# A constant of the cross-attention output added by VectorE, and one softmax pass over 16 heads

## The reference

```python
x = x + _L0_attn_ref(_layernorm(x), w_qkva, gamma)            # gated linear scan over the 1024 tokens
x = x + _L0_xattn_ref(_layernorm(x), ctx, Wq, Wkv, null_kv, Wout, ln_scale, ln_bias)
x = x + _L0_ffn_ref(_layernorm(x), w_gate, w_up, w_down)      # silu(gate) * up, both quantised, then down
```

```python
k = concatenate((nk, k)); v = concatenate((nv, v))            # 65 keys and values for each head
attn = softmax(q @ k.T)                                       # max over 65 scores, exp, sum, divide
out = (attn @ v) reshaped to (tokens, 16 * 64) @ Wout         # 256 channels
out = (out - mean) * rsqrt(var + 1e-6) * ln_scale + ln_bias
```

## Time and profile before

| what | value |
|---|---|
| median of 3 runs | 495.2 us |
| the profiled execution's own time | 493.31 us |
| its span | 491.5 us |
| between span and time | 1.8 us |
| PE busy | 461.3 us |
| DVE busy | 402.8 us |
| ACT busy | 329.0 us |
| POOL busy | 308.8 us |
| granted clock, mean share of full speed | 0.994 |

### The profile page before, as it was taken

How to read it: one execution, slowest core, us unless ns; L and a number is a source line. 1 busy time by engine, 2 the same in 40 slices (tenths; PEclk the granted TensorE clock), 3 DMA queues, 4 the chain that set the end, 5 groups by cost and what they waited for, 6 DMA issues and landing times.

```text
span 491.5 us, 7915 instructions
## 1 busy us (share of the span) xinstructions
PE 461.3 (94%) x2504; PEld 361.7 (74%) x2532; DVE 402.8 (82%) x882; ACT 329.0 (67%) x429; POOL 308.8 (63%) x465
## 2 busy tenths in 40 slices
PE   1999999999999999999999999999999999999673
PEld 0777888787677788777778777878878777786432
DVE  4689988974555688998989989899898998997785
ACT  4556644144544344898888888889788888887551
POOL 2234555741011478897788787787877878888860
PEclk9999999999999999999999999999999999999989
DMA  8997000240000000012131121212222121222243
GB/s 261 325 373 280 3 0 1 43 87 1 1 1 1 1 0 7 12 27 59 39 54 40 39 59 39 55 39 44 54 44 49 40 58 40 44 49 60 48 107 98
DMA packets 67129, 31.72 MB, mean 65 GB/s; under 512 B 49680, under 2 KB 65296, under 8 KB 67088
## 3 DMA queue, kind: packets, MB, share of 16 engines
q1 hardware_dynamic: 67088, 31.21, 25.2%
HBM read 15.21 MB, written 4.19 MB: 39 GB/s over the span
## 4 chain that ended last, share of the span: by engine, by line
PE 83%; DVE 6%; POOL 5%; issue 2%; DMA 2%; ACT 2%; SPq 0%; POOLq 0%; DVEq 0%; ACTq 0%
PE psum L1285 37%; PE psum L1301 12%; PE psum L1564 10%; PE psum L1559 10%; PE psum L1536 3%; PE psum L1544 2%; PE psum L1389 2%; PE psum L1425 2%; PE psum L1406 2%; PE psum L1320 2%; PE psum L1336 1%; DMA gcol<-in_L_attn_gamma_dram 1%; DVE region_a L1008 1%; DVE region_c L1111 1%; PE psum L1556 1%
## 5 line engine op out<-in xcount | busy, mean ns | idle before, releaser
L577 POOL TENSOR_TENSOR region_d<-region_d,rden 128x1024 f32<-128x1024 f32 x30 | 57.1, 1904 | 13.4 <-DVE rden L1087 13.1
L1559 PE MATMUL psum<-VW,region_d 128*128 128x256 f32 x256 | 60.6, 380 | 0.2
L1564 PE MATMUL psum<-VW,region_d 128*128 128x256 f32 x256 | 60.5, 379 | 0.0
L1071 DVE TENSOR_REDUCE mx<-psum 128x8 f32<-128x512 f32 x64 | 44.0, 687 | 14.3 <-PE psum L1285 13.2
L1285 PE MATMUL psum<-Mhi,xT2hi 128*128 128x512 f32 x128 | 53.8, 420 | 0.7 <-DVE xT2lo L1053 0.6
L1564 PEld LDWEIGHTS psum<-VW,region_d 128*128 128x128 f32 x256 | 48.6, 190 | 6.6
L1111 DVE SCALAR_TENSOR_TENSOR region_c<-psum,hzw,region_c 128x1024 f32<-128x1024 f32 x32 | 41.1, 1283 | 12.9 <-ACT region_c L791 12.7
L1559 PEld LDWEIGHTS psum<-VW,region_d 128*128 128x128 f32 x256 | 46.3, 190 | 6.5 <-ACT region_d L862 0.6
L1285 PE MATMUL psum<-Mhi,xT2lo 128*128 128x512 f32 x128 | 50.3, 393 | 0.0
L1285 PE MATMUL psum<-Mlo,xT2hi 128*128 128x512 f32 x128 | 50.0, 390 | 0.0
L1076 DVE SCALAR_TENSOR_TENSOR region_d<-mx,psum 128x512 f32<-128x512 f32 x60 | 40.9, 681 | 1.0
(11 more groups left out here) (160 smaller groups left out, 1164.3 us busy)
## 6 DMA issues: line engine op xcount, KB each, us to landing
out_dram<-xs SPq DMA_DIRECT2D x32, 128.0 KB, 1.9
xs<-in_x_dram SPq DMA_DIRECT2D x1, 2560.0 KB, 13.2
VW<-in_L_xattn_Wkv_dram SPq DMA_DIRECT2D x1, 2048.0 KB, 12.9
region_b<-in_L_xattn_Wkv_dram SPq DMA_DIRECT2D x1, 2048.0 KB, 16.8
xs<-in_x_dram SPq DMA_DIRECT2D x3, 512.0 KB, 6.7
region_w<-in_L_ffn_w_gate_dram SPq DMA_DIRECT2D x2, 512.0 KB, 9.6
region_w<-in_L_ffn_w_up_dram SPq DMA_DIRECT2D x2, 512.0 KB, 7.8
region_w<-in_L_ffn_w_down_dram SPq DMA_DIRECT2D x8, 128.0 KB, 5.7
```

Source lines behind the costliest of these rows:

```text
L577: pool.tensor_tensor(p_of(t).rearrange("p (h j) -> p h j", j=MK), e[:, :, 0:MK], rden[:, v, :].unsqueeze(2).broadcast_to([P, H, MK]), ALU. ...
L1071: dve.tensor_reduce(mx[:, hh, :], scores, AX.X, ALU.max).then_inc(max_done, 1)
L1559: pe.matmul(bank(7, D), pT[:, pair, :], VW[:, batch(n), pair, :], start=False, stop=False)
L1564: mm = pe.matmul(bank(7, D), pT[:, pair, :], VW[:, batch(n), pair, :], start=False, stop=pair == HC - 1)
```

## The change

The product of `ones_r` and `vnull` on PE goes. `vnull` becomes a plain float32 tile with the whole constant in all 128 rows (`nvsel` gets the null value in all its columns, and the subtraction L1102, the constant `ones_r` and a zeroing go). DVE adds `vnull` to bank 7 on the way to `y2` and takes the statistics from `y2`; ACT's `norm_out` works in place in `y2`. PE waits for DVE's addition of the tile before (`out_whole`) and no longer for ACT's normalisation (`y2_ready`). The wait on `x2_done` moves from ACT to DVE. In steps 5 to 29 (tiles 7 to 31) one `softmax_whole` stands for two `softmax_half`: one maximum over two banks, one null column, one subtraction, after both halves of the scores.

```diff
--- before.py
+++ after.py
@@ -77,8 +77,7 @@
 
 
         NR = P
-        vnull = sbuf("vnull", [NR, D], F32R)
-        ones_r = sbuf("ones_r", [NR, P], F32R)
+        vnull = sbuf("vnull", [NR, D])
         wgT = sbuf("wgT", [P, KD, FI], BF16)
         wuT = sbuf("wuT", [P, KD, FI], BF16)
         wdT = sbuf("wdT", [P, FC, D], BF16)
@@ -259,7 +258,6 @@
         wqT0_ready = sem("wqT0_ready")
         wqT1_ready = sem("wqT1_ready")
         nulls_negated = sem("nulls_negated")
-        nvsel_zero = sem("nvsel_zero")
         wout_summed = sem("wout_summed")
         fT_psum = sem("fT_psum")
         kvT_ready = sem("kvT_ready")
@@ -271,8 +269,8 @@
         xT2_lo_ready = sem("xT2_lo_ready")
         nv_set = sem("nv_set")
         vnull_psum = sem("vnull_psum")
-        vnull_hi = sem("vnull_hi")
         vnull_ready = sem("vnull_ready")
+        out_whole = sem("out_whole")
         absum_done = sem("absum_done")
         tot_psum = sem("tot_psum")
         wscale_done = sem("wscale_done")
@@ -510,8 +508,6 @@
                 pool.affine_select(out=t[:, :], in_=t[:, :], compare_op=ALU.not_equal, fill=1.0, base=0,
                                    pattern=[[-1, P]], channel_multiplier=1).then_inc(ident_set, 1)
             pool.memset(ones[:, :], 1.0).then_inc(consts_set, 1)
-            pool.memset(ones_r[:, :].bitcast(F32), 1.0).then_inc(consts_set, 1)
-            pool.memset(nvsel[:, :], 0.0).then_inc(nvsel_zero, 1)
             pool.wait_ge(consts_set, 2)
 
             def rounded(i):
@@ -546,9 +542,7 @@
                     rounded(2)
 
             groups(stage1)
-            pool.wait_ge(nvsel_zero, 1)
-            for row in (0, DH // 2):
-                pool.tensor_copy(nvsel[:, row:row + 1], nulls[:, 1:2]).then_inc(nv_set, 1)
+            pool.tensor_copy(nvsel[:, :], nulls[:, 1:2].broadcast_to([P, NR])).then_inc(nv_set, 1)
             pool.wait_ge(wout_loaded, 16)
             pool.wait_ge(q_psum, NG)
             pool.tensor_tensor(wsum, wout[:, 0, :], wout[:, 1, :], ALU.add).then_inc(wout_summed, 1)
@@ -774,9 +768,7 @@
             def norm_out(n, v):
 
                 act.wait_ge(nmr3_done, n)
-                if positive(n - 2):
-                    act.wait_ge(x2_done, n - 2)
-                act.activation(y2[:, v, :], bank(7, D), ACT.Identity, bias=sc3[:, v, 2:3],
+                act.activation(y2[:, v, :], y2[:, v, :], ACT.Identity, bias=sc3[:, v, 2:3],
                                scale=sc3[:, v, 1:2]).then_inc(y2_ready, 1)
 
 
@@ -841,7 +833,7 @@
             xT2_pair(1, 1)
             put_kvT(HC + 7)
             act.wait_ge(vnull_psum, 1)
-            act.activation(vnull[:, :], psum[0:NR, 7, 0:D], ACT.Copy).then_inc(vnull_hi, 1)
+            act.activation(vnull[:, :], psum[0:NR, 7, 0:D], ACT.Copy).then_inc(vnull_ready, 1)
             norm2(4, 0)
             put_values_second(3)
 
@@ -1076,6 +1068,20 @@
                 dve.scalar_tensor_tensor(out=e[:, :, 0:MK], in0=mx[:, hh, :].unsqueeze(2).broadcast_to([P, HB, MK]),
                                          scalar=0.0, in1=scores, op0=ALU.max, op1=ALU.subtract).then_inc(sim_sub, 1)
 
+            def softmax_whole(n, u):
+
+                scores = banks(0, 2).rearrange("p b (h j) -> p (b h) j", j=MK)
+                e = e2[:, u, :].rearrange("p (h j) -> p h j", j=J)
+                largest = mx[:, :, :].rearrange("p r h -> p (r h)")
+                dve.wait_ge(sim_psum, 2 * n + 2)
+                dve.wait_ge(shift_done, n)
+                dve.wait_ge(p_ready, n - 1)
+                dve.tensor_reduce(largest, scores, AX.X, ALU.max).then_inc(max_done, 2)
+                dve.wait_ge(max_done, 2 * n + 2)
+                dve.tensor_scalar(e[:, :, MK], largest, 0.0, None, ALU.max).then_inc(shift_done, 1)
+                dve.scalar_tensor_tensor(out=e[:, :, 0:MK], in0=largest.unsqueeze(2).broadcast_to([P, H, MK]),
+                                         scalar=0.0, in1=scores, op0=ALU.max, op1=ALU.subtract).then_inc(sim_sub, 2)
+
             def exp_sum(n, slot):
 
                 dve.wait_ge(exp_done, n + 1)
@@ -1097,10 +1103,6 @@
                     put_values_first(1)
             put_values_first(2)
             xT2_lesser(1, 1)
-            dve.wait_ge(vnull_hi, 1)
-            row = slice(DH // 2, DH // 2 + 1)
-            dve.tensor_tensor(vnull[row, :], psum[row, 7, 0:D], vnull[row, :].bitcast(F32), ALU.subtract) \
-                .then_inc(vnull_ready, 1)
             put_values_first(3)
 
             def hidden_layer(n, v):
@@ -1183,13 +1185,13 @@
             def stages2_3(n, u4):
                 u, v = u4 % 2, 1 - u4 % 2
                 head = isinstance(n, int) and n < 5
-                if exists(n + 2, T):
+                if exists(n + 2, T) and n < 5:
                     softmax_half(n + 2, 0, u)
+                elif exists(n + 2, T):
+                    softmax_whole(n + 2, u)
                 if head and n > 0:
                     exp_sum(n + 1, v)
                     exp_sum_reciprocal(n + 1, v)
-                if exists(n + 2, T) and not filling(n):
-                    softmax_half(n + 2, 1, u)
                 if filling(n):
                     softmax_half(n + 2, 1, u)
                 if u == 1 and exists(n, T - 3):
@@ -1212,7 +1214,13 @@
                 if exists(n, T):
 
                     dve.wait_ge(out_psum, n + 1)
-                    dve.bn_stats(st3[:, :], bank(7, D)).then_inc(st3_done, 1)
+                    if n == 0:
+                        dve.wait_ge(vnull_ready, 1)
+                    if n > 1:
+                        dve.wait_ge(x2_done, n - 1)
+                    dve.tensor_tensor(y2[:, u, :], bank(7, D), vnull[:, :], ALU.add).then_inc(out_whole, 1)
+                    dve.wait_ge(out_whole, n + 1)
+                    dve.bn_stats(st3[:, :], y2[:, u, :]).then_inc(st3_done, 1)
                     dve.wait_ge(st3_done, n + 1)
                     dve.bn_aggr(mv3[:, u, :], st3[:, :]).then_inc(mv3_done, 1)
                 if n < T - 1:
@@ -1286,7 +1294,7 @@
                 return mm
 
             pe.wait_ge(ident_set, 4)
-            pe.wait_ge(consts_set, 4)
+            pe.wait_ge(consts_set, 3)
 
             def stage1(g, u):
                 v = 1 - u
@@ -1411,7 +1419,7 @@
 
             def null_values():
 
-                pe.wait_ge(nv_set, 2)
+                pe.wait_ge(nv_set, 1)
                 pe.wait_ge(wout_summed, HC - 1)
                 pe.matmul(psum[0:NR, 7, 0:D], nvsel[:, :], wsum, start=True, stop=True).then_inc(vnull_psum, 1)
 
@@ -1549,14 +1557,13 @@
                     gate_up(n, v)
                 if exists(n, T):
 
-                    if positive(n):
-                        pe.wait_ge(y2_ready, n)
                     if n == 0:
                         pe.wait_ge(vnull_ready, 1)
-                    pe.matmul(bank(7, D), ones_r[:, :], vnull[:, :], start=True, stop=False)
+                    else:
+                        pe.wait_ge(out_whole, n)
                     pe.wait_ge(pT0_ready, n + 1)
                     for pair in range(HC // 2):
-                        pe.matmul(bank(7, D), pT[:, pair, :], VW[:, batch(n), pair, :], start=False, stop=False)
+                        pe.matmul(bank(7, D), pT[:, pair, :], VW[:, batch(n), pair, :], start=pair == 0, stop=False)
                 if exists(n, T):
 
                     pe.wait_ge(pT1_ready, n + 1)
```

## The result

The changed kernel takes 496.29 us (median of 20 runs, 495.1 to 498.24); the kernel before, beside it, 495.38 us (20 runs, 492.2 to 496.39). The ratio is 1.0031, with a 95% interval of 1.0019 to 1.0043. By the ratio it is 1.5 us slower, by the two medians 0.9: inside what was called no change, where 3.5 us less was forecast. The profiled execution of after has a span of 495.1 us and a time of 496.92. That of before was 2.1 us under its own median, so the two traces differ by more (3.6 us of span) than the medians.

What follows compares the result with a forecast made beforehand. The prediction took PE's work to bound the loop; -3.1 (loop), -0.6 and -0.6 (filling) and +0.8 (drain) made -3.5 us on 493.3, 489.8, or 491.7 us with 1.9 added for the median; range 488.0 to 498.0.

Steps and rivals of the forecast that it cites:

- the loop: Steps 5 to 29: a pair of steps falls from 20.18 to 19.93 us, giving -3.1 us over 12.5 pairs.
- the filling: Early steps: five products saved, -0.6 us, and PE's idle time in step 1 gone, another -0.6 us.
- the drain: From tile 29's statistics on: DVE's addition makes them later, costing +0.8 us.
- What bounds the kernel: Tiles' loop: PE's work sets the pace, 19.89 of 20 us; DVE and ACT have some 2 us to lose.
- What leaves PE: Product L1556 removed from PE: 0.21 us saved in each of steps 5 to 29.
- the later row: Trace of L1556 in a later step, behind a bf16 product: read as holding PE for 0.31 us.
- the filling row: Trace of L1556 in a filling step: the next product starts 0.12 us behind it.
- What DVE gets: DVE per step: addition about 0.46 us with its wait, merged pass saves 0.28 us, net 0.18 us more.
- The order: Odd step: DVE starts at 3.05 us, after both score halves; the lateness makes PE wait 0.17 us at the gates.
- B: Rival, loop: waits eat the gain, 493 to 494.5 us, 496 at worst; chance 0.30 shared with another rival.
- C: Rival, loop: POOL's queue carries DVE's lateness over ACT to PE's gates, 499 us; chance 0.18.

Runs made afterwards that it cites:

- e4: Kernel before with ACT's normalisation for the pair of transposes moved, in even steps, from the step's end to its start: ratio 0.9973 to the kernel before, pair 20.04 us.
- e1: Changed kernel with two half passes in all steps, so only the constant moves from PE to DVE: ratio 0.9957 to the kernel before, pair 20.02 us.
- e6: Kernel before without the product L1556 and nothing in its place (output lacks the constant): ratio 0.9923 to the kernel before, pair 20.01 us.
- e3: Changed kernel with ACT's normalisation for the pair of transposes moved, in even steps, from the step's end to its start: ratio 0.9942 to the kernel before.
- e10: Changed kernel with PE making the down product of tile n-7 before the pair of transposes in even steps: ratio 0.9961 to the kernel before, pair 19.96 us.
- e9: Changed kernel with half passes in even steps and the merged pass in odd steps only: ratio 1.0016 to the kernel before, pair 20.29 us.
- e5: Changed kernel with half passes in all steps and ACT's normalisation for the transposes early in even steps: 490.6 us, ratio 0.9904 to the kernel before.

## Why the prediction was wrong

The forecast was 491.7 us; 496.3 was measured. It lies in the range, on the side of the rivals. Of the forecast's terms the loop was to give -3.1 us and took 2.3 more (steps 5 to 28, one stray 0.39 included), the filling was to give -1.2 and gave -0.74, and the drain's +0.8 can't be told from its scatter. Point by point:

- **What bounds the kernel** was read too simply. "The pair is bound by PE's work" holds for the odd step. In the even one PE's load already waited 0.29 us for ACT's L756, and e4 shows that this cost 0.1 us. A busy share of 19.89 in 20 us does not tell a bound from two engines in step.
- **What leaves PE.** The term was 0.21 us in each step; the trace has 0.98 us from the first gate product to L1559 before (347.90 - 346.92) and 348.91 - 348.05 = 0.86 after: 0.12 us. The start of L1556 had hidden it: four gate products need 0.86 us, and its start stands 0.67 behind the first. The figure that the Trainium skill has for single products (0.11 us, page TensorE: Matmul & The Clock Gate, section Back-to-back issue gap) was nearer than my reading of the later row, and the filling row that agreed with it was the one to use. Even this shortens only the odd steps, as ACT holds the even ones (e1, e6). Over 12.5 pairs that is 0.13 x 12.5 = 1.6 us instead of the forecast's 5.2 before waits.
- **What DVE gets** was right: addition 0.41 us, maximum 1.22, subtraction 1.21. Statistics from SBUF take 0.43 us and not 0.42. The gain of an estimated 0.06 us, worked out from the TRN2 errata section of the Trainium skill's page VectorE: DVE Perf Modes, is not there. Left out was that the null columns would get shorter, by 5.5 us in all.
- **The order** was laid out nearly right as far as it went. The addition starts at 10.47 us on the odd step's clock (10.70 forecast), ACT's normalisation at 12.95 (346.72 - 333.77; 13.19), the second copy ends at 14.53 (14.76). At the gates PE's load then waits 0.2 us for that copy, where 0.17 was forecast, and the products lose nothing by it; only in step 6 did the gates hold them. The residual that was to hold the transposes into bank 5 for 0.12 us holds them in only one even step from 250 to 440 us of after (24); in e3 and e10, where it does so in every other even step, it costs 0.24.
- **The step that failed** is the next one: "In its queue behind it stand the two copies of the transposed probabilities." The list stops there. Behind the copies stand a table load, silu, the quantisation and two normalisations, and the last of them is read by PE's transposes at the end of the even step. I followed the queue to the first instruction on which PE waits and took it for the only one. The row of waits for L1425 was there to be read. The wait that took the product's place is 0.42 us in each even step, where the sum had 0.17 once in each pair, at the gates; e3, e10 and e9 show it from three sides. So both terms of "A pair takes 20.18 - 0.42 + 0.17 = 19.93 us" were wrong: the product took 0.12 to 0.13 off PE's work in each step, 0.25 in a pair, and the wait rose by 0.42 - 0.05 = 0.37 in each even step, which makes 20.18 - 0.25 + 0.37 = 20.30.
- **The filling** was right in kind and place; the 0.60 us are gone. Step 1 is 1.06 us shorter than before (6.98 and 8.04), but steps 2 and 4 are longer by 0.32 and 0.22, as ACT's normalisation, later by the addition, holds the copy that the output products need. That leaves 0.74 of 1.2 us.
- **The drain** is 1.67 us longer in the one pair of traces, from step 29 on, and was to be 0.8 longer. The mean of the eight traces with the addition is 0.7 above that of the four without, with a scatter of 3.4 us among the eight: neither number is confirmed.
- **The rivals.** B's outer end, 496 us with all of the loop's gain gone, was nearest in size, for its own reason (a longer chain) only in part; its smaller product, 0.12 us, was right. C had the right kind, a queue that carries DVE's lateness, but named POOL's; POOL waited for DVE 0.67 us ahead of the deviation and never held it.

## What to carry to other kernels

When an instruction is delayed, follow its engine's queue to the end of the step and ask of each instruction behind it who waits for it and with how much room; the first meeting is not always the tightest. An engine that is busy throughout may be in step with another one: look for instructions of its that start right behind another engine's end (0.05 us here), and at the rows of its weight loads, before promising that less work will shorten it. Merging two passes saves their fixed cost, but it gives up the start on the first half; do it where the engine arrives late anyway, and first look whether a small piece of work can be moved into another engine's idle time. Here that gave 0.3% on the kernel before (e4), 0.5% on top of the addition (e5 beside e1, by their ratios) and 0.9% on the changed kernel (e3), and the merged pass gave nothing.

## What the runs showed of the hardware

- The null column of step 1 on DVE ended 0.04 us behind POOL's running instruction in both traces, 1.73 us long behind a product and 0.34 behind an addition: shifting POOL's queue by half a microsecond against it changed it fivefold. Over all steps the mean of the null columns went from 455 ns to (6.5 + 1.6) / 30 = 270 ns. The exclusive lock that the Trainium skill describes (page SBUF - State Buffer, section SBUF: two separate sides) fits these ends; what a DVE instruction of this kind cost here depended on what POOL had running.
- The start of a matmul in the trace is not the end of the one before. L1556 cost 0.12 us where the next start stood 0.31 behind its own; only the distance between the same two neighbours with and without it gave its price.
- A weight load can wait without its product losing time: 0.2 us at the gates of after cost nothing, 0.29 us ahead of the transposes of before went with 0.13 for a pair (e4). A waiting load is a reason to look, and the distance of the products, or an edit, gives the price.
- In e3 and e10 the loop settled into a pattern of four steps, with pairs of 20.29 and 19.62 us in turn by DVE's statistics. A loop's time has to be taken over more than one pair.
